# The last layer's experts: rows scattered by expert during attention, plain block loads, results scattered to six planes

## What is computed

```
shared  = relu2(x @ w_up_shared) @ w_down_shared              # 512 wide
scores  = sigmoid(x @ gate_w.T);  scores_b = scores + gate_bias
grp     = sum of the two best scores_b in each of 8 groups of 8 experts
masked  = scores_b where the group is one of the 4 best, else -inf
eidx    = top_k(masked, 6);  w = scores[eidx] / (sum + 1e-20) * 2.5
routed  = sum over the six e of  w_e * (relu2(x @ w1[e]) @ w2[e])    # 128 wide
x       = x + shared + routed
```

## Time and profile before

| | us |
|---|---|
| three runs | 1116.10, 1113.84, 1114.15 |
| profiled execution | 1114.21 |
| its span, first to last instruction | 1112.4 |
| TensorE busy | 920.0 (83%) |
| VectorE busy | 593.4 (53%) |
| ScalarE busy | 349.0 (31%) |
| GpSimd busy | 338.6 (30%) |
| DMA: 118.56 MB, of it written 15.20 MB | mean 107 GB/s |

### The profile page before, as it was taken

One profiled execution on the slowest core, in us unless ns is written; L12 is line 12 of the kernel. 1 busy time (PEld: TensorE's weight loads), 2 busy tenths in 40 slices (PEclk: granted clock), 3 DMA queues, 4 the chain that ended last, 5 costly groups with the idle time before them and its releaser, 6 DMA issues. The chain is left out here.

```text
span 1112.4 us, 15899 instructions
## 1 busy us (share of the span) xinstructions
PE 920.0 (83%) x5294; PEld 582.5 (52%) x5306; DVE 593.4 (53%) x1290; ACT 349.0 (31%) x762; POOL 338.6 (30%) x409
## 2 busy tenths in 40 slices
PE   4799886999996689998999897997999885999500
PEld 2555543565654565655567553444557653777300
DVE  3878523676679652224586311113686574777533
ACT  2345542323321232221323221221333233666200
POOL 1135561122233230001033224002133204777276
PEclk9999997999998799997999998999899997999855
DMA  8000005211000200005200495778000294776343
GB/s 290 1 1 1 1 1 191 72 40 36 1 1 0 67 1 1 0 1 189 67 1 1 169 389 203 273 285 279 30 1 1 118 455 139 205 204 197 117 123 113
DMA packets 40639, 118.56 MB, mean 107 GB/s; under 512 B 7665, under 2 KB 25905, under 8 KB 38129
## 3 DMA queue, kind: packets, MB, share of 16 engines
q1 hardware_dynamic: 29024, 61.17, 15.9%
q10 hardware_dynamic: 4432, 36.98, 8.2%
q0 software_dynamic: 7104, 19.41, 6.5%
HBM read 102.32 MB, written 15.20 MB: 106 GB/s over the span
## 5 line engine op out<-in xcount | busy, mean ns | idle before, releaser
L1559 PE MATMUL fold_q_ps<-L1q_XT,L1q_M 128*128 128x512 f32 x192 | 94.1, 619 | 13.7 <-ACT fold_ab L1609 12.2
L1960 POOL DMA_INDIRECT g_pairs<-xd,moe_tok x80 | 77.3, 966 | 69.9 <-DMA xd<-L23w_xn 44.9
L1966 POOL DMA_INDIRECT L23w_xn<-ys,moe_slot x56 | 53.0, 947 | 104.7 <-DMA ys<-moe_y 71.0
L1677 DVE TENSOR_TENSOR g_pairs<-fold_q_ps,L1q_tab 128x512 f32<-128x512 f32 x96 | 59.5, 681 | 31.3 <-PE fold_q_ps L1559 31.3
L2099 PE MATMUL moe_ps<-f_wb,moe_hT 128*64 x256 | 63.8, 379 | 1.1 <-ACT moe_hT L2226 0.8
L2101 PE MATMUL moe_ps<-L23w_XT,moe_hT 128*64 128x256 f32 x256 | 63.8, 379 | 0.0
L300 PE MATMUL L_u_ps<-L_wffn,L_fT 128*128 128x512 f32 x128 | 59.6, 599 | 0.0
L1217 PE MATMUL af_ps<-L1q_XT,L1q_qw 128*128 128x512 f32 x128 | 57.6, 593 | 0.0
L1559 PEld LDWEIGHTS fold_q_ps<-L1q_XT,L1q_M 128*128 128x128 f32 x192 | 35.4, 195 | 34.2 <-issue 33.8
L1321 DVE TENSOR_TENSOR af_hid<-af_sg,af_ps 128x512 f32<-128x512 f32 x16 | 11.0, 687 | 76.2 <-ACT af_sg L1265 76.2
L1718 POOL TENSOR_TENSOR fold_step<-fold_minus_q,fold_sc 128x512 bf16<-128x512 bf16 x12 | 13.9, 1155 | 117.5 <-DVE fold_minus_q L1699 117.5
(11 more groups left out here) (427 smaller groups left out, 2201.7 us busy)
## 6 DMA issues: line engine op xcount, KB each, us to landing
moe_wa_second<-in_L_wa SPq DMA_DIRECT2D x12, 1024.0 KB, 4.9
ys<-g_pairs SPq DMA_DIRECT2D x80, 128.0 KB
g_pairs<-in_L_wa SPq DMA_DIRECT2D x8, 768.0 KB, 7.1
L23w_XT<-in_L_wb SPq DMA_DIRECT2D x12, 512.0 KB, 5.8
f_wb<-in_L_wb ACTq DMA_DIRECT2D x1, 4096.0 KB, 36.5
lat_more<-in_L_wa SPq DMA_DIRECT2D x4, 768.0 KB, 6.2
moe_wa_second<-in_L_wa SPq DMA_DIRECT2D x4, 768.0 KB, 5.7
fold_wa<-in_L_wa SPq DMA_DIRECT2D x3, 896.0 KB, 4.6
```

The source lines that it names most:

```text
L1559: mm = nc.tensor.matmul(q_ps[:, n % 2, x, :], F.M[:, g % 2, ic, x, c * P:(c + 1) * P], XT[:, ic, half * BANK:(half + 1) * BANK], start=ic ...
L1677: return nc.vector.tensor_tensor(dst.rearrange("p (b t) -> p b t", b=2), q_ps[:, p, x, :].rearrange("p (b t) -> p b t", b=2), F.tab[:, c, ...
L1960: nc.gpsimd.indirect_dma_start(out=x[:, n % R, :], out_offset=None, in_=xd, in_offset=bass.IndirectOffsetOnAxis(ap=tok[:, n:n + 1], axis=0 ...
L1966: nc.gpsimd.indirect_dma_start(out=rows[:, c % RR, :], out_offset=None, in_=ys, in_offset=bass.IndirectOffsetOnAxis(ap=slot[:, c:c + 1], a ...
```

## The change

Lines added sit in `layer0`, `roped_scores`, `latent` and in a new function `sorted_layer`, which replaces the second call of `routed_layer`.

- A table `sorted` in device memory has 65 rooms of 1024 rows, one room for each expert and one more; a row has 264 floats (1056 bytes): the token's 256, then a number that names token and choice. SP fills it with zeros beforehand, in 65 DMAs of 1.08 MB (70.3 MB in all): 28 in layer 0's block, two under way at a time, and 37 at the end of SP's list in `roped_scores`, where SP then waits until all have landed.
- In layer 3's attention, each tile is routed as soon as its scores exist: DVE picks six experts (`choose`), TensorE counts who came before (`place`), DVE turns that into row numbers (`rank`, `find_slots`), ACT makes six copies of the tile's rows (`copy_rows`), and POOL scatters them into `sorted`, six indirect DMAs of 128 rows (`send_rows`).
- `sorted_layer`: the sends of the last two tiles stand first in POOL's list. SP waits for all sends, then loads each tile as two plain blocks of 64 rows. The first 32 tiles take the first 64 rows of experts 2n and 2n+1 and need no register and no copied weights; the other 48 take what is over. Weights come in four parts. ACT reads each row's number, POOL scatters each tile's 128 results to their place in `results` (token by token, six rows each); empty rows are left out. When all have landed, SP loads `results` in eight DMAs of 786 KB into `planes`, and DVE adds six planes for each tile.
- Layer 2 keeps a buffer less (`up` lies in `sg`, with one wait more).

```diff
+ROOM, WIDE, TOP = 1024, 264, 6
+SORTED = 65 * ROOM
+FILL0 = 28
+def clear_rows(sp, G, i):
+    sp.dma_start(G.sorted[i * ROOM:(i + 1) * ROOM, :].rearrange("(p r) x -> p r x", p=P),
+                 G.zero[:].unsqueeze(1).to_broadcast([P, ROOM // P, WIDE])).then_inc(G.filled[i % 2], 16)
@@ layer0, sync
+                sp.wait_ge(l1_loaded, 64)
+                sp.wait_ge(cleared, 1)
+                for i in range(FILL0):
+                    need(sp, G.filled[i % 2], 16 * (i // 2))
+                    clear_rows(sp, G, i)
@@ roped_scores, sync
                     if g == 1:
                         old.clear(sp)
+                for i in range(FILL0, SORTED // ROOM):
+                    clear_rows(sp, G, i)
+                wait_cleared(sp, G)
+def send_rows(nc, pool, G, slot, flat, t):
+    rows = flat[:, 0:2 * TOP * WIDE].rearrange("p (q k x) -> p q k x", q=2, k=TOP)
+    for k in range(TOP):
+        nc.gpsimd.indirect_dma_start(out=G.sorted, out_offset=bass.IndirectOffsetOnAxis(ap=slot[:, t, k:k + 1], axis=0),
+                                     in_=rows[:, t % 2, k, :], in_offset=None).then_inc(G.sent[t % 2], 16)
@@ latent, tensor
+        def place(t):
+            pe.wait_ge(chose, t + 1)
+            pe.wait_ge(shifted, min(t + 5, NT))
+            pos = s_ps[:, 2 * (t % 2), 0:64]
...
+            mm = nc.tensor.matmul(pos, early.tri16[:], early.chosen[:, t, :], start=True, stop=t == 0)
+            for s in range(t):
+                mm = nc.tensor.matmul(pos, early.ones16[:], early.chosen[:, s, :], start=False, stop=s == t - 1)
+            mm.then_inc(placed, 1)
             if live(t - 2):
                 rate(t - 2)
+            if routed(t - 3):
+                place(t - 3)
@@ latent, scalar
+        def copy_rows(t):
+            act.wait_ge(normed2, t + 1)
...
+                act.wait_ge(G.sent[t % 2], 16 * TOP * (t // 2))
+            nc.scalar.copy(early.rows[:, t % 2, :, 0:D], xn[:, t, :].unsqueeze(1).to_broadcast([P, TOP, D])).then_inc(copied, 1)
@@ latent, gpsimd
+            if routed(t - 4):
+                if t == 4:
+                    wait_cleared(pool, G)
+                send(t - 4)
+        if early is not None:
+            send(NT - 3)
@@ latent, vector (choose has 12 steps on one tile, a drain between them)
+            link(nc.vector.tensor_scalar(v, v, 1.0, None, ALU.add))
+            link(nc.vector.reciprocal(v, v))
+            link(nc.vector.tensor_tensor(early.lg, v, G.bias[:], ALU.add))
+            for g in range(8):
+                ins = nc.vector.max(early.gtop[:, g, :], early.lg[:, 8 * g:8 * g + 8])
...
+        def find_slots(t):
+            dve.wait_ge(ranked, t + 1)
+            dve.wait_ge(copied, t + 1)
...
+            if routed(t - 3):
+                rank(t - 3)
             if live(t + 2):
                 shift(t + 2)
             if live(t - 1):
                 norm2(t - 1)
             if live(t + 5):
                 stats(stat1, sm1, t + 5)
+            if routed(t - 2):
+                choose(t - 2)
+            if routed(t - 3):
+                find_slots(t - 3)
@@ sorted_layer, sync
+                for s in range(2):
+                    sp.wait_ge(G.sent[s], 16 * K * NT // 2)
+                for n in range(NTL):
...
+                    need(sp, ids_kept, n - R + 1)
+                    for h in range(H):
+                        if n < FIXED:
+                            rows = G.sorted[(2 * n + h) * ROOM:(2 * n + h) * ROOM + SUB, :]
+                        else:
+                            rows = G.sorted[bass.ds(starts[h][n], SUB), :]
+                        sp.dma_start(x[h * SUB:(h + 1) * SUB, n % R, :], rows).then_inc(loaded[n % R], 16)
+                for s in range(YR):
+                    sp.wait_ge(stored[s], 16 * (before[s] + len(range(s, NTL, YR))))
+                for t in range(NT):
+                    sp.dma_start(planes[:, t].rearrange("p k d -> p (k d)"),
+                                 results[t * P * K:(t + 1) * P * K, :].rearrange("(p k) d -> p (k d)", k=K)).then_inc(got[t], 16)
@@ sorted_layer, gpsimd
+                for t in range(NT - 2, NT):
+                    send_rows(nc, pool, G, slot, flat, t)
+                nc.gpsimd.memset(ones16[:], 1.0)
+                nc.gpsimd.memset(oneP[:], 1.0)
+                nc.gpsimd.tensor_tensor(incl16[:], G.tri[0:E, 0:E], G.ident[0:E, 0:E], ALU.add).then_inc(const, 1)
+                for n in range(NTL):
+                    pool.wait_ge(ids_kept, n + 1)
+                    pool.wait_ge(y_kept, n + 1)
+                    nc.gpsimd.indirect_dma_start(out=results, out_offset=bass.IndirectOffsetOnAxis(ap=ids[:, n:n + 1], axis=0),
+                                                 in_=y[:, n % YR, :], in_offset=None,
+                                                 bounds_check=TOK * K - 1, oob_is_err=False).then_inc(stored[n % YR], 16)
@@ sorted_layer, tensor
+                s_make(0)
+                s_make(1)
+                s_fold(0)
+                count()            # waits for const
+                s_make(2)
...
@@ sorted_layer, scalar
+                for s in range(PARTS):
+                    part = slice(s * E // PARTS, (s + 1) * E // PARTS)
...
+                        act.dma_start(dst, a[name][:, s * E * D // PARTS:(s + 1) * E * D // PARTS]).then_inc(w_got[s], 16)
@@ sorted_layer, vector, at the end
+                for t in range(NT):
+                    dve.wait_ge(got[t], got_before[t] + 16)
+                    for k in range(K):
+                        c = t * K + k
+                        if c:
+                            dve.wait_ge(added, c)
+                        nc.vector.scalar_tensor_tensor(out=G.X[:, t, :], in0=planes[:, t, k, :], scalar=weight[:, c:c + 1], in1=G.X[:, t, :],
+                                                       op0=ALU.mult, op1=ALU.add).then_inc(added, 1)
```

399 lines of the change are left out of this document (386 added, 13 removed).

## The result

The changed kernel takes 1149.07 us (median of four runs, 1146.36 to 1155.07) against 1114.32 (four runs, 1113.84 to 1116.10): ratio 1.0316, interval 1.0271 to 1.0361. It is slower by 35 us. 1123 was forecast, so the direction was right and the size was not: +9 forecast, +35 measured. The median lies 0.9 us inside the upper end of the forecast's range, 1150.

What follows compares the result with a forecast made beforehand. TensorE carried most of the chain of waits, with a 43.48 us token store as one DMA link. Fills 8, attention 39, dispatch -7, loop 0, combine -31 gave +9: span 1121, so 1123 us, range 1094 to 1150.

Steps and rivals of the forecast that it cites:

- rival C: Fills at the end of roped_scores: slower than plain transfers, 140 us, +31 instead of +8, total 1146 us; chance 0.13.
- A: Whole kernel, the forecast itself: 1123 us, its own range 1110 to 1135; chance 0.45.
- fills: End of roped_scores: 37 zero fills at 342 GB/s take 117 us, +8; lower bound 0, upper +50.
- attention: Layer 3's attention: routing and sending each tile ends it at about 920 instead of 881.0, +39; bounds +27 and +50.
- tile loop: Loop over 80 tiles: TensorE keeps 1.345 us a tile, so 0; lower -3, upper +20.
- the ring: Layer 3's attention: shift, norm2, choose, place and score wait for one another, 11.5 us a step against 8.6.
- the tail: End of layer 3's attention: POOL sends six tiles from about 860, 45 us plus scalings and powers, until about 915.
- Dispatch: From attention's end to the tile loop: 48 us replace 54.9, -7; bounds -14 and +2.
- rival D: Tile loop: POOL's scatter or SP's two issues set the pace, 1.6 us a tile, +20, total 1143; chance 0.10.
- Combine: After the last copy: plane loads and 48 adds take 36 to 38 us in place of 68.9, -31.
- Rival B: Layer 3's attention: choose near 2.0 us, POOL's sends alone set its end, +27; total 1101 to 1108; chance 0.32.

Runs made afterwards that it cites:

- e1: Changed kernel with 44 instead of 28 of the fills in layer 0's block, sixteen fewer at the end of roped_scores: 1177.33 us, ratio 1.0346, disturbed call.
- e4: Changed kernel with epsilon's addition moved from GpSimd to VectorE in layer 3's attention, leaving GpSimd one power instruction: 1186.38 us in a disturbed call, attention 158.0 us.
- e3: Changed kernel with three small GpSimd instructions for constants put ahead of the last block's twelve scatters: 1195.55 us, in a disturbed call.
- e7: Changed kernel with constants ahead of the scatters and three weight quarters issued only after all scatters landed: 1194.45 us, beside 1190.03 unedited.
- b1: Changed kernel with 44 early fills, place behind score, one GpSimd power, constants first, three weight quarters late, some row loads on ACT: 1173.52 us, ratio 1.0281.

## Why the forecast was right in direction and short by 26 us

The range (1094 to 1150) holds 1149.07, and that is luck. Its upper end was put there for rival C, which didn't come true; the forecast's own range, A, ended at 1135, and A had attention at +45 at most and nothing for the tile loop. Three terms that were each too small, fills, attention and tile loop, filled the room that C had been given.

- Fills, +8 against 12.0: the rate came out right (342 against 336 GB/s) across two measures, as said above; the block needed 123.6 us for what I put at 120, and 0.4 came ahead of it. e1 shows the whole of it, and 2.5 us in the next stages that the sum lacked.
- Attention, +39 against 45.2: two terms were too small. One is "`place` 0.5, `score` 3.65" in the ring, taken at full clock. With the waits of the ring the granted clock fell, and `score` took 6.70 and 5.37 us, 4.8 us in sum; by the clock of before, step 6 began at 881.4 and not at 879, so 2.4 us were left of it there, and the first scatter left at 862.5 and not at 860. The other is the tail, sized with 0.55 for the powers: a drain behind scatters made the pair 2.4 us (e4), and the sends of six tiles took 59.4 us from the first start to the last end, forecast 55. `choose` at 4.3 and the scatter at 1.25 were right.
- Dispatch, -7 against -4.7: as forecast, the rows of x came last (e3); four tiles of them were needed and not one.
- Tile loop, 0 against +11.5: this is the largest miss. The step that failed is "two loads a tile, 0.33 us each at least, with registers and waits some 1.0". 0.33 is the issue of a load that stands alone; back to back a load takes 0.64 even with a plain address, and with register loads and long issues the two took 1.6 us a tile from tile 32 on. It was rival D with half its price; POOL, at 1.27 of 1.345, was not the bound.
- Combine, -31 against -29.8: right. It takes 37.3 us from the last copy, forecast 36 to 38; the forecast set that against 68.9, a window that begins 1.8 us ahead of that copy, where 67.1 was due.
- Rival B fell with `choose` at 4.39 and attention at +45.2; rival C with 123.6 us for the fills, where it had 140 and the landing.

## What to carry to other kernels

Work that is cheap on a full batch can be dear when cut into tiles and put into a pipeline: here 4.39 us a tile for 2.0. Where another engine's list names it ahead of its main work, the whole ring slows, and here TensorE's clock fell with it. Count the instructions of each queue per tile, the one that only issues DMAs too, against the pitch of the loop, and take the cost of an issue from a place where several stand back to back, not from a lone one. Here two loads a tile left SP no slack against 1.345 us, and the register loads made it the bound, though the busy times of the page don't count SP's issues. A wait that holds back a load also holds back all that stands behind it on the issuing engine; e7, b1 and b4 paid for that.

## What the hardware showed

- Back to back, a load leaves SP every 0.64 us with a plain address and every 0.65 with one from registers, and every 0.80 us on average over the 96 with register loads among them. Single issues of either kind took up to 1.9 us (L2651).
- A drain on GpSimd right behind six scatters takes 2.89 us, 1.7 more than the longest without scatters; a single instruction behind them isn't delayed (e4).
- TensorE's granted clock was 0.79 in the step behind a wait of 3.57 us, and a matmul group of 3.65 us took 6.70 there.
- Row loads and scatters beside weight packets: scatters land 30 us after the block's start beside 16.8 MB in 16 KB packets, 18 beside a quarter of it.
- The same kernel's tile loop took 109 us in one hour and 152 in another, with all other stages within 3 us.
